# Unused TensorE products in the waits of a mixture stage and a sparse stage

## What is computed

```python
x = x + _layernorm(_L0_attn_ref(_layernorm(x), ...))   # causal attention, 16 heads of 16, f32
x = x + _layernorm(_L0_ffn_ref(_layernorm(x), ...))    # mixture: router picks 128 tokens per image,
                                                       # attention and gated FFN on these alone
x = x + _layernorm(_L1_attn_ref(_layernorm(x), ...))   # sparse: 35 queries per head attend, the rest get
                                                       # the mean of the values
x = x + _layernorm(_L1_ffn_ref(_layernorm(x), ...))    # FFN 256 -> 1024 -> 256, dequantized weights
```

## Time and profile before

| | us |
|---|---|
| median of 3 runs | 2781.16 |
| lowest, highest | 2778.76, 2781.85 |
| profiled execution | 2780.3 |
| its span, first to last instruction | 2778.3 |
| TensorE busy (matmuls) | 2515.5 |
| VectorE busy | 1739.7 |
| ScalarE busy | 1180.4 |
| GpSimd busy | 895.5 |
| mean granted TensorE clock | 0.957 |

### The profile page before, as it was taken

The page is one execution under the profiler, slowest core; times in us unless marked ns, Lnnn a source line. Parts: engine busy times, 40 slices in busy tenths (PEclk is TensorE's granted clock), DMA queues, the critical chain, the costliest instruction groups (busy, mean ns, idle before and its releaser), DMA issues. The chain is left out here.

```text
span 2778.3 us, 40505 instructions
## 1 busy us (share of the span) xinstructions
PE 2515.5 (91%) x14196; PEld 1494.4 (54%) x14196; DVE 1739.7 (63%) x4778; ACT 1180.4 (42%) x1885; POOL 895.5 (32%) x1420
## 2 busy tenths in 40 slices
PE   5999999999999999999857999976999999999997
PEld 2444444454444444444436888843666666666664
DVE  6767576676868678778759664736544444454452
ACT  2556666656566665566623332121232223222311
POOL 4040523507153260621251221114324415325241
PEclk8899999999999999999967999988999999999999
DMA  5252350514326062331220222321102102011010
GB/s 172 63 161 56 114 147 25 183 56 160 102 76 185 25 184 56 131 115 53 76 90 24 73 94 89 115 92 62 47 17 76 62 16 76 18 61 47 24 38 31
DMA packets 150140, 228.65 MB, mean 82 GB/s; under 512 B 18757, under 2 KB 114961, under 8 KB 141650
## 3 DMA queue, kind: packets, MB, share of 16 engines
q1 hardware_dynamic: 145842, 222.04, 25.6%
q0 software_dynamic: 4096, 4.01, 0.5%
HBM read 113.75 MB, written 112.27 MB: 81 GB/s over the span
## 5 line engine op out<-in xcount | busy, mean ns | idle before, releaser
L1137 ACT ACTIVATE pt<-ps 128x1024 f32<-128x1024 f32 (+3 forms) x768 | 600.3, 811 | 306.4 <-PE ps L1033 211.3
L931 DVE CUSTOM_DVE_ANT_0 masked<-ps,mask_q 128x128 bf16<-128x128 f32 (+3 forms) x1024 | 473.1, 485 | 183.4 <-PE ps L1009 181.3
L1009 PE MATMUL ps<-sk,sq 96*128 96x512 bf16 (+3 forms) x1536 | 429.5, 337 | 57.7 <-DVE mx L931 16.7
L935 DVE TENSOR_REDUCE mx<-ps 128x1 f32<-128x512 f32 x512 | 351.6, 687 | 93.4 <-PE ps L1009 92.9
L1030 PE MATMUL ps<-sq,sk 99*128 99x512 bf16 (+3 forms) x1536 | 399.0, 329 | 12.0 <-DMA sq<-scratch_nm_parts 10.2
L1009 PEld LDWEIGHTS ps<-sk,sq 96*128 96x128 bf16 x1536 | 132.2, 97 | 376.4 <-DVE mx L931 98.9
L1049 PE MATMUL ps<-pt,val 128*32 128x512 f32 (+3 forms) x3072 | 328.5, 500 | 3.0 <-ACT yt L1145 3.0
L1030 PEld LDWEIGHTS ps<-sq,sk 99*128 99x128 bf16 x1536 | 147.5, 98 | 157.1 <-ACT pt L1137 55.1
L2414 PE MATMUL ps<-w_fc,eyb 128*128 128x256 f32 x1024 | 227.3, 380 | 2.3 <-ACT eyb L2468 2.3
L2402 PE MATMUL ps<-w_xr,w_fc 128*128 128x512 f32 x512 | 224.3, 596 | 1.5 <-ACT w_xr L2458 1.5
L2468 ACT ACTIVATE eyb<-ps,w_fc_b 128x512 f32<-128x512 f32 x128 | 88.0, 687 | 304.4 <-PE ps L2402 296.6
(11 more groups left out here) (343 smaller groups left out, 4339.2 us busy)
## 6 DMA issues: line engine op xcount, KB each, us to landing
scratch_stacks<-space SPq DMA_DIRECT2D x32, 768.0 KB, 4.2
sq<-scratch_stacks SPq DMA_DIRECT2D x32, 768.0 KB, 8.7
sk<-scratch_stacks SPq DMA_DIRECT2D x32, 768.0 KB, 9.5
scratch_stacks<-space SPq DMA_DIRECT2D x32, 512.0 KB, 5.0
scratch_x<-w_xr SPq DMA_DIRECT2D x16, 1024.0 KB, 7.8
space<-in_L_attn_x SPq DMA_DIRECT2D x8, 1024.0 KB, 14.0
scratch_stacks<-space SPq DMA_DIRECT2D x32, 256.0 KB, 6.1
w_xr<-in_L_attn_x SPq DMA_DIRECT2D x8, 1024.0 KB, 6.3
```

Source lines behind the costliest of these rows:

```text
L931: nc.vector.tensor_tensor_reduce(mem["masked"][:, slot, 0:n], ps[:, RING[slot], 0:n], mem["mask_q"][:, BANK - n:BANK], 1.0, -3e38, ALU.add ...
L935: nc.vector.reduce_max(mx[:, hh, i, half:half + 1], ps[:, RING[slot], 0:n], AX.X)\
L1009: nc.tensor.matmul(ps[:, bank, 0:n], sq[0:ROWS, h, i * P:(i + 1) * P], sk[0:ROWS, h, half * BANK:half * BANK + n], start=True, stop=True)\
L1137: nc.scalar.activation(pt[:, u % 3, 2 * pair:2 * pair + 2, 0:n], ps[:, bank:bank + 2, 0:n], ACT.Exp, scale=SCALE).then_inc(e["exp_done"], 1)
```

## The change

Before nine steps of the mixture stage and five steps of the sparse stage, TensorE makes a number of products of the identity with itself, 128x128 in f32, into the bank that the step is about to write. Nobody reads them: the step's first product starts the bank anew. In the mixture stage they come after the wait for the bank and before the wait for the data. In the sparse stage they come before all waits of the step, into bank 0 (before `kt`), bank 2 (before `base`) or bank 6 (before the three `pt`), banks that nobody reads at that time. The counts are 117 and 86. Nothing else is changed.

```diff
+IDLE_IN_MIXTURE = {
+    ("hnt", 0): 32, ("s", 0, 0): 6, ("pt", 0, 0): 18, ("pt", 0, 1): 8, ("o", 0): 10, ("pt", 1, 0): 5, ("pt", 1, 1): 8,
+    ("hnt2", 1): 18, ("hnt2", 2): 12,
+}
+IDLE_IN_SPARSE = {("kt", 0, 0, 0): (0, 24), ("base", 1): (2, 36), ("pt", 1, 2): (6, 6), ("pt", 1, 3): (6, 10), ("pt", 1, 4): (6, 10)}
+
+
+def idle_products(nc, w, into, n):
+
+    for _ in range(n):
+        nc.tensor.matmul(into, w["ident"][:, :], w["ident"][:, :], start=True, stop=True)
...
                 if uses:
                     pe.wait_ge(taken, uses)
+                if step in IDLE_IN_MIXTURE:
+                    idle_products(nc, w, into[:, 0, 0:P] if kind in PAIR_STEPS else into[:, 0:P], IDLE_IN_MIXTURE[step])
                 if kind == "flat":
...
             for step in order:
                 kind, b, a = step[0], step[1], step[2:]
+                if step in IDLE_IN_SPARSE:
+                    bank, n = IDLE_IN_SPARSE[step]
+                    idle_products(nc, w, ps[:, bank, 0:P], n)
                 if kind == "qx":
```

## The result

The changed kernel takes 2776.61 us (median of 18 runs, 2766.03 to 2781.91), the kernel before, run beside it, 2781.82 (18 runs, 2776.67 to 2785.69): a ratio of 0.9980, 95% interval 0.9971 to 0.9988, which is 3.3 to 8.1 us off. The forecast was 2776.6. Beside the last group of experiments two executions of the kernel before took 2961 and 4190 us, at a mean clock of 0.85 and 0.55; they are left out of every median and ratio.

What follows compares the result with a forecast made beforehand. TensorE's clock pays only where its time lies on the path; VectorE bounds the mixture stage up to 1541 us, then TensorE. Terms 0 + 0.6 + 0 + 0 + 1.6 + 0.6 + 0.9 + 0.9 = 4.6 us off 2781.16: 2776.6, range 2771.5 to 2781.

Steps and rivals of the forecast that it cites:

- (a): 32 products before the mixture stage's first tile and 6 before its first scores: 0, VectorE waits for GpSimd's factor anyway.
- (c): Mixture stage, 10 products before the 17-column products, 5 and 8 in the next image: 0 to 1.1 us, taken 0.
- (d): Mixture stage, 18 products before `hnt2` of image 1: 0, since VectorE is the bound there.
- (b): Mixture stage, 18 and 8 products before the first two groups of 8 transposes: 0 to 0.9 us gain, taken 0.6.
- (e): Mixture stage, 12 products before the tile at 1541.41 us: 0 to 1.6 us gain, taken 1.6 as the clock holds.
- rival 2: Clock falls in the remaining idle time, or dips only move: 0 to 2 us off, 2780 us; chance 0.17.
- (f): 24 products before the sparse stage's first keys: faster keys against a possibly late end, net gain taken 0.6 us.
- The forecast's sign: At (f), products end after the load lands: 1.2 us late if the clock rises after 3 us.
- (g): Sparse stage, 36 products before the second image's mean product: a third of 2.6 us, 0.9 us gain.
- (h): Sparse stage, 6, 10, 10 products before the second image's last three transpose groups: a quarter of 3.5 us, 0.9 gain.
- 1: Rival: the clock holds everywhere, 11.4 us off, 2769.8 us; chance 0.20.
- 3: Rival: products run at the low level and end late, 7.2 us more, 2788.4 us; chance 0.05.

Runs made afterwards that it cites:

- off_path: Changed kernel with only the places (a), (c), (d) kept and no products in the sparse stage: 2781.0 us, ratio 1.0002 to the kernel before.
- filled: Changed kernel with higher counts at (b), (e), (f), (g), (h), filling each wait almost to its end: 2779.31 us, ratio 0.9988 to the kernel before.
- first_image_too: both_filled plus 10 products before the fourth group of transposes of the sparse stage's first image: 2771.14 us, ratio 0.9967 to the kernel before.
- late_filled: Changed kernel with 10, 19, 26 products in place of 6, 10, 10 at (h): 2772.92 us, ratio 0.9966 to the kernel before.
- sparse_only: Changed kernel with only the 86 products of the sparse stage: 2777.57 us, ratio 0.9984 to the kernel before.
- late_only: Kernel before plus only 12 products of 512 columns at (g) and 10, 19, 26 products at (h): 2774.04 us, ratio 0.9978.
- mix_only: Changed kernel with only the 117 products of the mixture stage: 2779.27 us, ratio 0.9990 to the kernel before.
- mean_long: Changed kernel with 12 products of 512 columns in place of the 36 at (g): one profiled execution, 2768.6 us, not timed otherwise.
- transposed: Changed kernel with each added product made a transpose of the identity, same counts: 2778.4 us, ratio 0.9991 to the kernel before.
- both_filled: Changed kernel with 12 products of 512 columns at (g) and 10, 19, 26 products at (h): 2771.58 us, ratio 0.9970 to the kernel before.

## Why the prediction was right, and which of its steps were not

**(a), (c), (d): 0, right.** off_path has these places alone and gains nothing, within its 2 to 3 us. For (a) the reason given, VectorE's wait for GpSimd, is the row at 1420.96 us: longer by what was won.

**(b): 0.6 forecast, 1.1 measured, every time.** All nine kernels with products here (40 and 20 of them in filled) have -1.01 to -1.14 in this column, the others -0.10 to +0.03. The step that was mis-sized is the bound: it took 1.94 against 1.07 us for the group and left out the transpose behind it, which is on the same path (0.42 us before, 0.27 after). The group also began 0.1 us earlier, counted from VectorE's row at 1420.96 (1422.58 before): 0.85 + 0.15 + 0.1 = 1.1 us. Nor did it fall out differently from one execution to the next, as I had said of each term.

**(e): 1.6 forecast, 0 in this profile.** The failed step is "The clock stayed at 1.00 over 1932 to 1935 us, in which TensorE was busy for 0.62 us only the earlier trace rows, a thinner stretch than the one left here: I take all of it, 1.6." A stretch in which the reading is 1.00 says only that the clock had not fallen yet; it does not say that the same idle time keeps it next time. Seven kernels have the same 12 products with the same 2 us idle behind them: in three the clock fell (5.1 us for L1819, a column of 0.1 or less), in four it held (3.62 us; 1.6 us won in three of them and 3.2 in one), 1.1 on average. In the eighth, first_image_too, TensorE came late as in filled, its products ended 1.1 us behind the tile, and 0.6 us was won. late_filled is one where it held:

```profile
1532.60 2.84 PE L1351 MATMUL ps<-w_ident 128*128 128x128 f32 x24
1537.43 0.44 PE L1706 MATMUL ps<-w_ident,hn 128*128 128x128 f32 x2 [1.99 <-DVE hn L1648]
1537.71 3.62 PE L1819 MATMUL ps<-space,cxnt 128*128 128x256 f32 x16
...
1629.15 4.31 PE L1772 MATMUL ps<-cval,cpt 128*128 128x17 f32 x32
1633.30 5.47 PE L1790 MATMUL ps<-hnt,space 128*128 128x128 f32 x24
```

Its last two rows show what came of it. Before, the same two steps were

```profile
1634.64 3.64 PE L1755 MATMUL ps<-cval,cpt 128*128 128x17 f32 x32
1638.13 2.92 PE L1773 MATMUL ps<-hnt,space 128*128 128x128 f32 x24
```

The clock falls during the products of 17 columns in some executions, with TensorE busy throughout, and the step behind them pays: 5.47 us for 2.92. In late_filled the stretch of 1630 to 1632 us still has 0.98, and then:

```profile
1632.00:1634.00 2.00, 2.00 (x11) 2.00 (x11) 0.65 (x4) 0.00 (x0) 1.28 (x5) 0.50 0.00 0
```

In all three kernels that won 1.61 us at (e), and in filled and first_image_too, this cost 3.2 to 3.5 us before 1817; in the others it was -1.5 to +1.4. That is rival 2 (a dip moves) at this one place, if the two are connected. Whether they are, or both only depend on when the stage begins, was not tried. Counted to 1817 us, the products of (e) have brought nothing that these runs show: columns e and rest together are +0.8 us on average in the eight kernels with 12 of them, and +0.6 in the four without (before at 0, sparse_only, off_path, late_only).

**(f): 0.6 forecast, 0.8 in this profile, 1.2 by the averages.** The eight kernels with 24 products average -0.46 there, and the four with none (before at 0, mix_only, off_path, late_only) +0.74: 1.2 us. The four lie far apart (-0.09 to +1.77), so the size is rough. The keys took 7.0 to 7.2 us in all eight, 8.7 to 10.2 without. The row of 24 took 5.60 us here and in mean_long, and 6.97 to 7.22 in the six others, near the 6.8 that the step had for a rise after 3 us. The forecast's sign, an end behind the landing of the load, did not show in this profile (5.60 us, then 1.07 idle), and did in five of those six.

**(g): 0.9 forecast, a loss of 0.35.** "A third" was a guess between a gap of 3 us and one of 4. With 36 products and 3.35 us behind them the clock fell in four executions out of four, and the low level then reached further into L2334 (8.86 to 9.21 us against 8.65). Filled with long products the place gives the 2.55 us that the forecast had as its end.

**(h): 0.9 forecast, 1.3 on average, 0.3 in this profile.** The five kernels with 6, 10 and 10 give 0.28, 0.16, 0.92, 3.22 and 1.80. Here the sentence that each term falls out differently holds. The rule against it that the prediction weighed, that transposes do not count as activity of TensorE the way products do (the Trainium skill, page "TensorE: Matmul & The Clock Gate", section "Part 4: PE-mode transpose"), isn't borne out here: transposes alone lifted the clock from 0.51 to 1.00 in transposed, and in late_filled it held through eight of them and 0.81 us of idle behind them. What lost the clock was the idle time around them.

**The sum.** With the columns' averages it is 1.1 + 0 to 1.1 + 1.2 - 0.35 + 1.3, 3.3 to 4.3 us, against 4.6 forecast and 3.3 to 8.1 measured. That the total came out was luck: two terms that were too large (e and g, 1.8 to 2.9 us together) met three that were too small (b, h, and f by its average: 1.5 us). **The rivals:** 1 (all places hold, 11.4 us off) is no property of the changed kernel, but both_filled comes near it, 8.3 us off (5.3 to 11.4). 3 did not happen. A stall of TensorE's stream, named as what would upset the sum, does exist, with 14 products more in (g); what causes it is open.

## What to carry to other kernels

Unused products pay reliably only when they fill the gap nearly to its end: with 2.0 us left at (e) the clock held in four executions of seven, with 3.4 us left at (g) in none of four, and with 1.2 us or less in every one (the mean's place four times, the last transposes five times). For a gap that would take more than some 80 short rows prefer few long products, as far as one place can tell, and count them for the shortest gap that the place ever has, since a late TensorE turns the same products into a delay (2.9 us at (e) in filled). And judge such a change by many runs and by one landmark sequence over several traces: the clock's dips in untouched code moved a single profile by more than the change.

## What the runs showed of the hardware that I had not expected

- At the mean's place some 80 short rows (one per 0.11 us) ran without a break, and then, as the loads of the second image set in (share 0.4 to 1.1), one product every 0.7 us, with waits put down to issue, until the clock went to 0.50; no packet of instructions on q8 fell into the stall. 12 products of 512 columns in their place did not stall, nor did 100 short rows at another place.
- The low level comes in untouched code as well, with TensorE busy: L1772 and the step behind it (0.50 over 1632 to 1634 us of late_filled). The start of the mixture stage lay between 3.9 us earlier and 3.7 us later than in the trace of before, in code that is the same in all kernels.
- A group of transposes of 4 us, nothing else on TensorE, brought the clock from the low level to the high one.
